# Three attentions: value products one key block behind the exponentials, with two buffers of them

## The reference, cut to what matters

```python
# layer 0, first attention: softmax over ALL keys, then a mask, then the values
p = softmax(q @ k.T / sqrt(s)); p = p * triu(ones); z = p @ v
# layer 0, second attention, and layer 1, first attention: causal
p = softmax(where(causal, q @ k.T * scale, -inf)); z = p @ v
```

## Time and profile before

| what | value |
|---|---|
| median of three executions | 2693.38 us (2685.63 to 2704.46) |
| the profiled execution, its own time | 2694.99 us |
| its span, first to last instruction | 2693.1 us |
| its mean granted TensorE clock | 0.895 of full speed |
| TensorE, VectorE, ScalarE, GpSimd busy | 85%, 70%, 52%, 13% of the span |
| `att0`, `att1`, `att2` | about 137 to 846, 988 to 1418 and 1730 to 2160 us |

### The profile page before, as it was taken

How to read it: one execution, slowest core, us unless ns; L and a number is a source line. 1 busy time by engine, 2 the same in 40 slices (tenths; PEclk the granted TensorE clock), 3 DMA queues, 4 the chain that set the end, 5 groups by cost and what they waited for, 6 DMA issues and landing times. The chain is left out here.

```text
span 2693.1 us, 40170 instructions
## 1 busy us (share of the span) xinstructions
PE 2297.7 (85%) x14544; PEld 1027.6 (38%) x14544; DVE 1897.4 (70%) x3935; ACT 1412.1 (52%) x2105; POOL 352.5 (13%) x559
## 2 busy tenths in 40 slices
PE   4799999999997469999985997699999968979896
PEld 2333333333332133333333443333333333644473
DVE  4788898889882568888853554688888458437644
ACT  1066677677775105667761222147677623853582
POOL 2000000000000010000120000100001214313430
PEclk8599999999999658999986998589999778989898
DMA  4310100000000150111230001501212224613460
GB/s 174 59 25 7 27 7 11 7 12 7 8 2 4 51 110 7 28 34 29 36 47 2 1 0 60 102 7 27 38 29 33 47 72 153 194 54 117 161 192 16
DMA packets 78397, 134.42 MB, mean 50 GB/s; under 512 B 16784, under 2 KB 39056, under 8 KB 76176
## 3 DMA queue, kind: packets, MB, share of 16 engines
q1 hardware_dynamic: 74912, 121.82, 18.3%
q10 hardware_dynamic: 3312, 10.33, 1.3%
HBM read 58.90 MB, written 13.63 MB: 27 GB/s over the span
## 5 line engine op out<-in xcount | busy, mean ns | idle before, releaser
L700 ACT ACTIVATE att_probs<-psum 128x1024 f32<-128x1024 f32 (+3 forms) x1152 | 1037.9, 951 | 619.5 <-PE psum L748 617.7
L658 DVE TENSOR_REDUCE att_part_max<-psum 128x1 f32<-128x512 f32 x1792 | 1127.5, 683 | 161.8 <-PE psum L730 158.1
L730 PE MATMUL psum<-k_rows,att_q_rows 64*128 64x512 f32 (+3 forms) x2304 | 819.4, 484 | 100.5 <-DMA att_q_rows<-q_pieces 52.9
L730 PEld LDWEIGHTS psum<-k_rows,att_q_rows 64*128 64x128 f32 x2304 | 360.8, 197 | 757.4 <-DVE att_part_max L658 534.6
L773 PE MATMUL psum<-att_probs,v_aug 128*9 128x512 f32 (+3 forms) x3712 | 446.3, 555 | 19.2 <-ACT att_z_sb L692 19.0
L748 PE MATMUL psum<-att_q_rows,k_rows 64*128 64x512 f32 (+3 forms) x2304 | 421.4, 408 | 13.5 <-ACT att_probs L700 9.2
L655 DVE CUSTOM_DVE_ANT_0 att_masked<-psum,mask_max_sb 128x384 bf16<-128x384 f32 (+3 forms) x512 | 232.8, 486 | 82.2 <-PE psum L730 77.4
L748 PEld LDWEIGHTS psum<-att_q_rows,k_rows 64*128 64x128 f32 x2304 | 240.1, 194 | 90.1 <-ACT att_probs L700 57.8
L608 POOL TENSOR_SCALAR_AFFINE_SELECT att_probs<-att_probs 128x256 f32<-128x256 f32 x256 | 102.5, 406 | 814.3 <-ACT att_probs L700 812.0
L769 PE MATMUL psum<-att_probs,att_one_only 128*9 128x512 f32 (+3 forms) x1280 | 147.8, 534 | 10.2 <-ACT att_z_sb L692 10.0
L614 POOL TENSOR_SCALAR_AFFINE_SELECT att_diag<-att_probs 128x256 f32<-128x256 f32 x128 | 50.3, 407 | 718.4 <-ACT att_probs L700 631.6
(11 more groups left out here) (249 smaller groups left out, 1985.2 us busy)
## 6 DMA issues: line engine op xcount, KB each, us to landing
k_rows<-k_pieces SPq DMA_DIRECT2D x96, 256.0 KB, 8.1
lproj_swapped<-lproj_other SPq DMA_DIRECT2D x128, 128.0 KB, 2.1
latt_k<-local_k_T SPq DMA_DIRECT2D x32, 384.0 KB, 3.0
att_q_rows<-q_pieces SPq DMA_DIRECT2D x168, 64.0 KB
lproj_table<-in_tables SPq DMA_DIRECT2D x16, 512.0 KB, 4.3
latt_q<-local_q_T SPq DMA_DIRECT2D x32, 256.0 KB, 2.4
latt_v_seen<-local_v_tok SPq DMA_DIRECT2D x64, 128.0 KB, 2.4
latt_v_seen<-local_v_tok SPq DMA_DIRECT2D x32, 256.0 KB, 2.4
```

The source lines that it names most:

```text
L658: nc.vector.tensor_reduce(column, ring[e % NRING][:, 0:w], AX.X, ALU.max).then_inc(ring_free, 1)
L700: nc.scalar.activation(probs[s % NPROBS][:, pr, :, at:BANK], st[pr][:, :, at:BANK], ACT.Exp, scale=scale).then_inc(st_free, 1)
L730: nc.tensor.matmul(ring[e % NRING][:, 0:w], q_rows[u % NQ][rows, pr, qt * P:(qt + 1) * P].bitcast(F32R), k_rows[b][rows, pr, kc * BANK:kc ...
```

## The change

Three edits, all in `attention()`, and so in all three calls:

- TensorE runs `products(s - 1)` in step s in place of `products(s - 2)`, and one call instead of two is left behind the loop.
- `NPROBS` is 2 instead of 3, so the exponentials of step s wait for `products(s - 2)` instead of `products(s - 3)`.
- `take_z` of the unit before is called in step f + 1 ahead of both exponentials, instead of in step f + 2 between the two.

```diff
-NPROBS = 3
+NPROBS = 2
...
                 if s >= NPROBS:
                     act.wait_ge(pv_done, s - NPROBS + 1)
+                if u > 0 and kb == 1:
+                    take_z(u - 1)
                 for pr in range(2):
                     act.wait_ge(st_full, 2 * s + pr + 1)
                     nc.scalar.activation(probs[s % NPROBS][:, pr, :, at:BANK], st[pr][:, :, at:BANK], ACT.Exp, scale=scale).then_inc(st_free, 1)
-                    if pr == 0 and u > 0 and kb == 2:
-                        take_z(u - 1)
             take_z(NU - 1)
...
                 maxima(plan.issued_by(u, (kb + 0.5) / plan.blocks[u]))
-                if s >= 2:
-                    products(s - 2)
+                if s >= 1:
+                    products(s - 1)
                 maxima(plan.issued_by(u, (kb + 1) / plan.blocks[u]))
-            products(NS - 2)
             products(NS - 1)
```

## The result

The changed kernel takes 2654.32 us in the median of four executions (2649.70 to 2655.40); the kernel before, run on the same chip, 2691.36 (2685.63 to 2704.46). The ratio is 0.9852, with a 95% interval of 0.9814 to 0.9891: 1.5% faster, 37.0 us. The forecast was 2664.

What follows compares the result with a forecast made beforehand. TensorE was taken to bound the attentions, VectorE close behind, with TensorE's waits for the copy removable. 31.8 - 2.9 - 1.2 + 2.6 = 30.3 us gave 2664 us; own range 2657 to 2671, 80% range 2648 to 2684.

Steps and rivals of the forecast that it cites:

- The stall in `att0`: At unit turns TensorE's waits for the copy vanish: 31.8 us in all calls; mid-`att0` units get 0.7 us shorter.
- rival C: VectorE at 84% is the true limit and TensorE waits for it instead: no change, 2693 us; chance 0.07.
- What ScalarE keeps: In six turns where ScalarE sets the pace the copy's 0.48 us stay: 2.9 us given back.
- rival B: ScalarE becomes the stall and all 45 turns pay 0.48 us: 9 us won, 2686 us; chance 0.17.
- The triangle: Products wait for GpSimd's triangle in four diagonal steps of each call's last unit: 1.2 us lost, at worst 4.9.
- The buffers: With two buffers, exponentials wait for `products(s - 2)`, a wait that ends 0.77 us early: costs nothing.
- rival D: The third buffer was needed and every step pays: slower, 2722 us at 0.1 us beyond the modelled end; chance 0.05.
- The clock: Clock drops behind the copy's wait in the causal calls go by half: 2.6 us won, bounds nothing and 5.2.
- four drops: Four causal turns with products of 1.6 us and more right behind the wait, 5.2 us in all.
- rival A: The clock comes back wholly, with two more drops a causal call: 10.4 us instead of 2.6, 2656 us; chance 0.17.

Runs made afterwards that it cites:

- experiment 3: The changed kernel with a third buffer (`NPROBS = 3`): 2654.22 us, ratio 0.9863.
- experiment 6: The changed kernel with every second maxima tile multiplied twice in the diagonal steps of the causal calls' first four units: 2652.71 us, ratio 0.9832.
- Experiment 2: The changed kernel with the copy between the two exponentials of step f + 1 instead of ahead of both: 2693.95 us, ratio 1.0005.
- Experiment 1: The kernel before with only the copy moved ahead of both exponentials of step f + 2; lag 2, three buffers: 2649.15 us, ratio 0.9842.
- 7: The changed kernel once more, unchanged, for a second trace: 2650.57 us, ratio 0.9835.
- 4: The kernel before once more, unchanged, for a second trace: 2693.62 us in one execution.
- 8: Experiment 1 once more, the kernel before with only the copy moved ahead: 2648.72 us, ratio 0.9819.
- 5: The changed kernel with three buffers, and lag 2 with the copy in step f + 2 in the causal calls' first four units: 2648.84 us, ratio 0.9814.

## Where the forecast was right and where it was not

The forecast's terms can be held against each stretch. A call's first exponentials and copies give the lengths of its units; the forecast is regrouped from its own terms by the place of each wait (10.0 us of TensorE's waits lay in `att0`, 1.6 in the rising units, 17.3 in the later ones; 0.07 us more for each).

| stretch | before, us | after, us | gain | gain by the forecast's terms |
|---|---|---|---|---|
| `att0` | 708.9 | 697.5 | 11.3 | 11.05 - 0.96 - 0.4 = 9.7 |
| rising units, `att1` and `att2` | 134.8 + 136.6 | 138.3 + 141.3 | -8.2 | 1.7 |
| later units, `att1` and `att2` | 294.9 + 296.7 | 278.2 + 278.9 | 34.6 | 18.9 - 1.9 - 0.8 + 2.6 = 18.8 |
| sum | | | 37.7 | 30.2 |

**The stall in `att0`: right, in mechanism and size.** The forecast's own point of failure was 0.7 us a unit. The starts of the third and fourth unit's exponentials, before and then after:

```profile
227.95 1.94 ACT L700 ACTIVATE att_probs<-psum 128x1024 f32<-128x1024 f32 x2 [0.75 <-PE psum L748]
...
272.89 1.94 ACT L700 ACTIVATE att_probs<-psum 128x1024 f32<-128x1024 f32 x2 [0.75 <-PE psum L748]
```

```profile
227.33 1.94 ACT L702 ACTIVATE att_probs<-psum 128x1024 f32<-128x1024 f32 x2 [0.74 <-PE psum L748]
...
271.56 1.94 ACT L702 ACTIVATE att_probs<-psum 128x1024 f32<-128x1024 f32 x2 [0.74 <-PE psum L748]
```

44.94 us became 44.23: 0.71. Over the first fourteen units the gain per unit is 0.38 to 0.90. So the gain was TensorE's own, and rival C (the stall is absorbed by VectorE) is out.

**What ScalarE keeps: too much taken.** The forecast gave back 2.9 us for six turns in which ScalarE sets the pace. The last two units of `att0`, two of the six, gained 1.21 and 0.74 us, not less than the others. (The last unit varies, though: 36.34 and 37.62 us in the two traces of the kernel before.) And the turn of the earlier trace rows lost less than was taken (ScalarE's and TensorE's rows, after):

```profile
1290.27 0.60 ACT L692 ACTIVATE att_z_sb<-psum 128x512 f32<-128x512 f32 x1
...
1290.74 4.05 ACT L702 ACTIVATE att_probs<-psum 128x1024 f32<-128x1024 f32 x4
...
1291.04 1.05 PE L773 MATMUL psum<-att_probs,v_aug 128*9 128x512 f32 x8
```

```profile
1290.00:1293.00 3.00, 2.58 (x19) 0.96 (x18) 1.78 (x6) 2.85 (x5) 0.00 (x0) 1.00 0.14 38
```

ScalarE goes on without a pause behind the copy, the products take 1.05 us instead of 1.89, and the 3 us around them run at the full clock, where the earlier trace rows had 0.52. The unit that holds this turn went from 27.01 to 25.01 us. In `att2`, where the same turn had the full clock before and after, the unit went from 25.63 to 25.01: 0.62 us for a wait of 0.84 removed, so some 0.2 us were kept there and not 0.48. ScalarE's pauses before the copy, which rival B needed, come to 5.6 us in seven places, 4.3 of it at the ends of the three calls. B is out: it asked for a loss in every turn.

**The triangle: small, as forecast, but not where it was put.** Products waited for GpSimd 1.4 and 0.9 us, 2.3 in all (the lines of the page above); 1.2 was taken, 5 was the point of failure. The forecast put its 1.2 us into the diagonal steps of the last units, and nothing behind the loop. In the trace the steps show one wait, of 0.19 us; the other three (0.88, 0.55 and 0.66 us) stand ahead of the last block of each call. That triangle has to be done before a call can end in either kernel, so whether they cost any time is not shown. The two of `att1`, after:

```profile
1390.48 0.62 PE L773 MATMUL psum<-att_probs,v_aug 128*9 128x256 f32 x8 [0.19 <-POOL att_probs L608]
1391.64 0.41 PE L773 MATMUL psum<-att_probs,v_aug 128*9 128x128 f32 x8 [0.55 <-POOL att_probs L608]
```

**The buffers: right, and rival D is out.** ScalarE's idle time before the exponentials is put down to scores and to nothing else in the loop (line 702, after), and experiment 3 with its third buffer gives the same time (0.1 us apart, where executions differ by several us):

```profile
  PE psum L748: 579.6, 518
  issue: 108.2, 3
```

The Trainium skill (Perfetto Trace Analysis, Identifying Performance Opportunities) says that a gap that repeats on the engine that should be saturated can mean too few buffers. For the buffers of the exponentials no run agrees with it: 2654.32 us with two, 2654.22 with three. The buffer that the products waited for was another, the bank `z_ps`, of which there is one; whether a second bank would have closed the gap as well was not tried. Moving one copy in a strict order closed it without one.

**The clock: the term that was mis-sized, in both directions.** The forecast took 2.6 us, half of four drops, with 5.2 as its bound, and rival A 10.4. In the later units the gain is 34.6 us, of which the removed waits are 18.9. At lag 1 a unit ends with one more block of products done, so the later units have one block of 256 columns fewer to do and the rising ones one more: about 0.6 us a call (0.62 for such a block at the full clock, in experiment 6), 1.2 in two. The remaining 14.5 us are more than five times what was taken. Not all of them need be the clock's: twelve of these 24 units ran at the full clock in both kernels, and they gained 12.5 us where 10.7 went by the waits. The windows of the twelve later units of `att1` and of `att2`, before:

```profile
1122.95:1417.87 294.92, 273.90 (x1865) 106.12 (x1863) 225.63 (x620) 207.35 (x253) 38.45 (x96) 0.95 0.23 38
1860.50:2157.25 296.75, 276.83 (x1865) 107.07 (x1863) 225.68 (x620) 207.78 (x253) 38.44 (x96) 0.94 0.23 38
```

and after:

```profile
1114.48:1392.70 278.22, 263.12 (x1857) 103.73 (x1855) 225.34 (x620) 207.03 (x253) 38.47 (x96) 0.99 0.25 40
1839.84:2118.71 278.87, 264.12 (x1857) 104.14 (x1855) 225.60 (x620) 207.03 (x253) 38.44 (x96) 0.99 0.25 40
```

The granted clock rose from 0.95 and 0.94 to 0.99, and with it TensorE's busy time fell by 23.5 us in the two; VectorE's and ScalarE's stayed. By the clock's record in the trace the time at the low level fell from 27.3 + 37.5 us to 3.4 + 6.8.

The step that failed is the count of the drops. The forecast found four turns with products of 1.6 us and more right behind the wait. The trace of the kernel before shows eleven, five in `att1` and six in `att2`, with products of 1.68 to 1.90 us behind waits of 0.40 to 0.84 us. In nine of them the clock falls within 0.5 us of the start of these products; in the last two of `att2` it is still low from the turn before. Three of the nine, before:

```profile
1392.68 1.89 PE L773 MATMUL psum<-att_probs,v_aug 128*9 128x512 f32 x8 [0.40 <-ACT att_z_sb L692]
...
2092.09 1.88 PE L773 MATMUL psum<-att_probs,v_aug 128*9 128x512 f32 x8 [0.76 <-ACT att_z_sb L692]
...
2112.64 1.90 PE L773 MATMUL psum<-att_probs,v_aug 128*9 128x512 f32 x8 [0.79 <-ACT att_z_sb L692]
```

At the forecast's own 1.29 us each, eleven are 14.2 us (an estimate from these rows), near the 12.7 to 14.5 that can be the clock's. Of the low clock, 44.4 of the 64.8 us lay in the last three units of the two calls, of four blocks each, where even A had put only two drops a call.

Two things made these drops, and the experiments part them. Experiment 2 keeps the wait and has lag 1: its later units take 288.6 and 291.8 us, 11.3 less than before, with 25.1 us at the low level instead of 64.8. Experiment 1 has no wait and lag 2: 278.5 and 282.4 us, with 17.1 us at the low level; its repeat 279.0 and 280.0, with 10.2. Either edit alone takes most of it away (one trace of experiment 2, two of experiment 1). So most of the low clock in the later units needed both the wait *and* what lag 2 puts beside it: at the turn of a falling unit lag 2 runs the narrow products of the last two diagonal blocks in the first steps of the next unit. That the narrow products are what matters there is argued from the order, not isolated by a run.

In the rising units it goes the other way, and this no part of the forecast had. Rows of TensorE at the end of the third unit of `att1`, before and then after:

```profile
1076.30 1.05 PE L773 MATMUL psum<-att_probs,v_aug 128*9 128x512 f32 x8
...
1077.62 0.56 PE L748 MATMUL psum<-att_q_rows,k_rows 64*128 64x128 f32 x4
...
1079.57 0.83 PE L773 MATMUL psum<-att_probs,v_aug 128*9 128x384 f32 x8
```

```profile
1066.28 0.83 PE L773 MATMUL psum<-att_probs,v_aug 128*9 128x384 f32 x8
...
1067.38 0.55 PE L748 MATMUL psum<-att_q_rows,k_rows 64*128 64x128 f32 x4
...
1069.64 1.04 PE L773 MATMUL psum<-att_probs,v_aug 128*9 128x256 f32 x8
```

On the diagonal every block is narrower than the one before it. With lag 2 the products ahead of the scores of 128 columns are 512 wide, with lag 1 only 384, and the next 256 instead of 384. In these steps TensorE waits for VectorE's maxima in either kernel, and between these waits it has fewer columns to multiply with lag 1. At 1068.57 the clock falls. The 10.07 us up to there and the 10.24 us after, in the changed kernel:

```profile
1058.50:1068.57 10.07, 8.82 (x53) 3.60 (x52) 8.96 (x24) 4.48 (x8) 2.63 (x7) 1.00 0.01 2
1068.57:1078.81 10.24, 10.23 (x49) 4.87 (x49) 7.47 (x18) 4.39 (x6) 0.57 (x2) 0.50 0.14 37
```

and at the same steps of the kernel before:

```profile
1068.52:1078.59 10.07, 8.81 (x53) 3.44 (x52) 8.75 (x24) 4.27 (x8) 2.44 (x6) 1.00 0.01 2
1078.59:1088.83 10.24, 9.10 (x61) 3.95 (x63) 8.99 (x21) 6.54 (x8) 0.77 (x2) 1.00 0.13 36
```

49 matmuls instead of 61 in the same time, at 0.50 instead of 1.00. TensorE's busy time ahead of the fall does not tell the two apart (8.82 and 8.81 us); what differs in the rows is the width of the products. The fourth unit, which follows, tells it best, because it comes behind these steps in every kernel. By windows over that unit, the clock is below 1.00 in all eight calls with lag 1 there (0.92 and 0.95 after, 0.97 and 0.92 in 7, 0.93 and 0.94 in 3, 0.96 and 0.88 in 2), and 1.00 in all ten with lag 2 (before, 4, 1, 8, 5). Lengths without the stall: 40.37 to 40.49 us with lag 2, 40.72 to 42.37 with lag 1, 1.3 us apart in the mean. Experiment 6 agrees: lag 1, with TensorE given more to do in these steps, and the full clock in both calls, shown here in `att1`.

```profile
1077.20:1118.20 41.00, 39.74 (x268) 16.08 (x266) 37.58 (x87) 28.86 (x34) 3.21 (x8) 1.00 0.04 10
```

The Trainium skill (TensorE: Matmul & The Clock Gate, Part 1) says that the clock follows how busy TensorE has lately been; experiment 6 agrees, as more work in the same steps kept the clock at 1.00; the busy time of the profile alone does not show it, since 8.82 and 8.81 us had different sequels. The rising units lost 8.2 us where 1.7 were to be gained. Of these 9.9, 1.7 lie in the first units (22.57 us instead of 21.72, at the low clock), which fits the block that moved across the border, 1.2 us at the full clock. Another 2.5 are the fourth units. The other 5.7 lie in the second and third units, where the clock varies between executions of one kernel (the third unit had 0 and 13.7 us at the low level in the two calls of the repeat 8), so how much of it belongs to lag 1 stays open. Over all traces the rising units of both calls take 271.4 to 278.3 us with lag 2 (five traces) and 275.3 to 282.9 with lag 1 (four, without experiment 6): on average 5 us apart, with ranges that overlap, so 8.2 is the difference of two executions and not the price of lag 1.

**Rival A** (the clock comes back wholly, 2656) was thus the nearest in number, and true of the later units; but it had neither the size there nor the loss in the rising ones. Net, the clock and what goes with it gave 14.5 - 8.7 = 5.8 us (8.7 is 9.9 less the 1.2 of the block; some 1.8 of the 14.5 may not be the clock's), 3.2 more than taken. With 2.7 that ScalarE and the triangle were to keep in the causal calls (what they did keep is already inside the 14.5) and 1.6 in `att0`, that is the 7.5 us between the table's sums. The number came out near in part by luck: a gain taken too small and a loss not foreseen offset each other.

What the three edits are worth: the whole gain is the copy's place ahead of both exponentials. Lag 1 by itself brings as much in the later units (11.3 us, experiment 2) as it loses in the rising ones (138.6 + 144.3 us against 134.8 + 136.6 before: 11.4, in one trace of each), and the times of the two kernels agree (2693.95 and 2694.83). The third buffer is spared at no cost.

## What to carry to other kernels

When an engine waits for a copy that another engine could have made sooner, look first at what stands just ahead of that copy in the strict order of its engine: here one place earlier was the whole gain, and the pipeline's depth by itself was worth none. A shift between stages also changes which wide matmuls stand beside which narrow ones; here, where TensorE already waited for another engine, the low clock came and went with that. Before pricing a wait on TensorE, go through every turn and count the low-clock time of the whole stretch, not only the long matmuls behind the waits of the rows at hand.

## What the runs showed of the hardware that was not expected

At the end of waits of 0.40 to 0.84 us TensorE's clock fell to half in nine turns of the kernel before. Most of the time at the low clock (64.8 us in the later units before, 10.2 in the changed kernel) went when the wait went, or when other work stood beside it (25.1 left in experiment 2); where one stretch of 3.4 us could be priced alone it cost 1.1 to 1.4 us. The clock also fell without any long idle time: in the changed kernel at 1068.57, where the waits of its matmuls in the 6 us before had been 0.4 us at most, and then it stayed low for 10.24 us of nearly gapless work (10.23 us busy). And a unit with eight more matmuls was 0.8 us shorter in the mean than without them (40.97 us against 40.72 to 42.37), with the clock at 1.00 instead of 0.92 to 0.97.
